# Decoder layer in fp32, one core: the last half batch of the feed-forward part in channel chunks and token tiles, the last batch's squares on another engine

## What is computed

```python
x = x + _L0_attn_ref(_layernorm(x), ...)
x = x + _L0_xattn_ref(ctx_1024, ctx_1024, _layernorm(x), ...)
x = x + _L0_ffn_ref(_layernorm(x), W_r, W_k, W_v, mu_r, mu_k)

# _L0_ffn_ref
x_prev = jnp.concatenate([jnp.zeros((B, 1, C), x.dtype), x[:, :-1, :]], axis=1)
xr = mu_r * x + (1.0 - mu_r) * x_prev
xk = mu_k * x + (1.0 - mu_k) * x_prev
r = jax.nn.sigmoid(jnp.einsum('btc,dc->btd', xr, W_r))
k = jnp.einsum('btc,dc->btd', xk, W_k)
k_act = jnp.square(jax.nn.relu(k))
out = r * jnp.einsum('btc,dc->btd', k_act, W_v)
```

## Time and profile before

| | us |
|---|---|
| median of 3 runs | 444.62 (443.23 to 445.12) |
| the profiled execution | 445.27 |
| its span, first to last instruction | 443.5 |
| TensorE busy | 427.9 |
| VectorE busy | 368.4 |
| ScalarE busy | 301.4 |
| GpSimd busy | 155.2 |

### The profile page before, as it was taken

How to read it: one execution, slowest core, us unless ns; L and a number is a source line. 1 busy time by engine, 2 the same in 40 slices (tenths; PEclk the granted TensorE clock), 3 DMA queues, 4 the chain that set the end, 5 groups by cost and what they waited for, 6 DMA issues and landing times.

```text
span 443.5 us, 8230 instructions
## 1 busy us (share of the span) xinstructions
PE 427.9 (96%) x2738; PEld 277.4 (63%) x2738; DVE 368.4 (83%) x672; ACT 301.4 (68%) x760; POOL 155.2 (35%) x200
## 2 busy tenths in 40 slices
PE   7999999999989999999999999999999999989888
PEld 5745463566546766576656685475665775568766
DVE  6788786979998889688999988799999888488875
ACT  4778986786796776657796577766877658428621
POOL 2171301137044343428242430734632532255410
PEclk9999999999999999999999999999999999979999
DMA  8668122715110002751103003443112000000001
GB/s 286 234 204 269 46 98 94 261 71 182 59 47 1 1 1 97 260 191 48 49 1 120 0 14 130 143 153 135 35 35 75 2 1 1 0 25 2 0 26 47
DMA packets 22177, 38.23 MB, mean 86 GB/s; under 512 B 2808, under 2 KB 7160, under 8 KB 21880
## 3 DMA queue, kind: packets, MB, share of 16 engines
q1 hardware_dynamic: 22136, 37.71, 25.1%
HBM read 23.02 MB, written 14.68 MB: 85 GB/s over the span
## 4 chain that ended last, share of the span: by engine, by line
PE 75%; DVE 9%; issue 6%; ACT 5%; POOL 3%; DMA 1%; SPq 0%; ACTq 0%; POOLq 0%; DVEq 0%
PE av_bank L913 22%; PE m_bank L845 8%; PE s_pair L899 8%; PE m_bank L849 6%; PE m_bank L1058 3%; ACT e_sb L1165 3%; PE m_bank L965 3%; DVE nmax L1369 3%; PE m_bank L1123 2%; PE m_bank L1070 2%; PE m_bank L1134 2%; PE m_bank L1145 2%; PE m_bank L983 2%; PE m_bank L930 1%; PE m_bank L1087 1%
## 5 line engine op out<-in xcount | busy, mean ns | idle before, releaser
L1165 ACT ACTIVATE e_sb<-s_pair,nmax 128x512 f32<-128x512 f32 x256 | 173.4, 690 | 61.6 <-DVE nmax L1369 59.8
L1369 DVE TENSOR_REDUCE nmax<-s_pair 128x2 f32<-128x1024 f32 x128 | 152.6, 1213 | 22.9 <-PE s_pair L899 21.8
L913 PE MATMUL av_bank<-e_sb,v_sb 128*64 128x512 f32 x512 | 119.0, 600 | 0.7 <-POOL v_sb L1649 0.7
L1649 POOL TENSOR_TENSOR v_sb<-v_sb,rsum 128x256 f32<-128x256 f32 x64 | 39.3, 617 | 140.4 <-DVE rsum L1377 135.7
L913 PEld LDWEIGHTS av_bank<-e_sb,v_sb 128*64 128x64 f32 x512 | 33.1, 136 | 61.6 <-issue 55.9
L899 PE MATMUL s_pair<-q_st,k_st 64*128 64x512 f32 x256 | 50.4, 457 | 3.3 <-ACT e_sb L1165 3.3
L1165 ACT ACTIVATION_READ_ACCUMULATOR e_sb<-s_pair,nmax 128x1 f32 x256 | 53.0, 207 | 0.0
L899 PEld LDWEIGHTS s_pair<-q_st,k_st 64*128 64x128 f32 x256 | 21.0, 184 | 36.7 <-ACT e_sb L1165 25.9
L1658 POOL TENSOR_TENSOR rstd<-veps,power 128x2 f32<-128x2 f32 x24 | 17.3, 719 | 58.6 <-DVE veps L1433 58.6
L845 PE MATMUL m_bank<-wo_hi,ot_hi 128*128 128x256 f32 x128 | 36.6, 291 | 0.0
L849 PE MATMUL m_bank<-wo_lo,ot_hi 128*128 128x256 f32 x128 | 34.9, 279 | 0.0
(11 more groups left out here) (182 smaller groups left out, 829.9 us busy)
## 6 DMA issues: line engine op xcount, KB each, us to landing
q_st<-q_parts SPq DMA_DIRECT2D x31, 256.0 KB, 3.4
k_st<-k_parts SPq DMA_DIRECT2D x31, 256.0 KB, 3.1
k_parts<-qkt_hi SPq DMA_DIRECT2D x7, 512.0 KB, 3.1
k_parts<-qkt_lo SPq DMA_DIRECT2D x7, 512.0 KB, 4.2
q_parts<-qkt_hi SPq DMA_DIRECT2D x8, 256.0 KB, 2.0
q_parts<-qkt_lo SPq DMA_DIRECT2D x8, 256.0 KB, 2.3
out<-x_sb SPq DMA_DIRECT2D x8, 256.0 KB, 2.2
x_sb<-in_x SPq DMA_DIRECT2D x3, 512.0 KB, 5.4
```

What stands on the lines that cost most here:

```text
L913: mm = pe.matmul(av_bank[n % AV_BANKS][64 * par:64 * par + 64, :], v_sb[:, m, 2 * p + par, :], e_sb[:, (4 * q + 2 * i + par) % E_RING, :], ...
L1165: act.activation(e_sb[:, g % E_RING, :], s_pair[k // 2][:, k % 2, :], ACT.Exp, bias=nmax[:, g % 8:g % 8 + 1], accum_out=esum[:, q % 4, k:k ...
L1369: dve.tensor_reduce(nmax[:, at:at + 2], s_pair[i][:, :, :], AX_X, ALU.max, negate=True)\
L1649: pool.tensor_tensor(v_sb[:, m:m + 2, 2 * p:2 * p + 2, :], v_sb[:, m:m + 2, 2 * p:2 * p + 2, :], rsum[:, q % 4, :].rearrange("p (m h) -> p ...
```

## The change

Seven edits, for batch 3, half 1 alone (`LAST_HALF`) unless said otherwise:

1. `t3` uses two banks, one for each channel chunk, and signals each when its two transposes are done; ScalarE copies each chunk by itself.
2. `mix` subtracts and mixes chunk by chunk, and signals `mixk_ready` after each; `mix_rec` signals `mixr_last` after each chunk.
3. `fk` uses two banks, one for each token tile, and has the input chunk c as its outer loop: 8 matmuls of 128 columns. Relu is applied tile by tile.
4. A new unit `frv` takes the place of `fr` and `fv` on TensorE: receptance then value products of tile 0, then of tile 1, in four banks.
5. tanh, gate, residual and store go tile by tile: two stores of 128 KB.
6. The squares of both halves of batch 3 are ACTIVATEs of Square on ScalarE, behind their relu; those of the other batches stay on GpSimd.
7. The seven warm-up matmuls at the end of TensorE's list go.

The diff, without the edits of the unit table (which drop the warm units at places 335 to 341, give `fr` and `fv` of (3, 1) no place of their own on TensorE, put `frv` at place 333, and drop the square units of batch 3 on GpSimd and VectorE):

```diff
@@ -29,7 +29,9 @@
 V_ON_DVE = (1, 3)
 X_TILES = 4
 
-BANKED = {"first", "t1", "qk", "v", "op", "t2", "kv", "kf", "z", "xs", "pt", "pv", "fc", "t3", "fr", "fk", "fv"}
+LAST_HALF = (B - 1, (1,))
+
+BANKED = {"frv", "first", "t1", "qk", "v", "op", "t2", "kv", "kf", "z", "xs", "pt", "pv", "fc", "t3", "fr", "fk", "fv"}
 
 
 UNITS = [
@@ -514,7 +510,9 @@
 
 def bank_units(name, b, args):
 
-    if name in ("xs", "z", "pv"):
+    if name == "frv":
+        return [(part, b, args + (t2,)) for t2 in range(2) for part in ("fr", "fv")]
+    if name in ("xs", "z", "pv") or (name in ("t3", "fk") and (b, args) == LAST_HALF):
         return [(name, b, args + (r,)) for r in range(2)]
     return [(name, b, args)]
 
@@ -722,6 +720,10 @@
 
             return xn[k > 1 or (b, half) == (0, 1)]
 
+        def is_last(b, half):
+
+            return (b, (half,)) == LAST_HALF
+
         def stacked(n):
 
             return n // STACK + (n % STACK != 0)
@@ -818,8 +820,14 @@
                 sp.dma_start(k_st[:, n % STACK, :].bitcast(F32), k_rows).then_inc(stack_in[1][n % STACK], 16)
 
             def fv(b, half):
+                t, at = b * NT + 2 * half, x_at(b, half)
+                if is_last(b, half):
+                    for t2 in range(2):
+                        sp.wait_ge(res_ready, 2 * b + half + 1 + t2)
+                        sp.dma_start(out.rearrange("(t p) d -> p t d", p=P)[:, t + t2, :], x_sb[:, at + t2, :])\
+                          .then_inc(res_out[half], 16)
+                    return
                 sp.wait_ge(res_ready, 2 * b + half + 1)
-                t, at = b * NT + 2 * half, x_at(b, half)
                 sp.dma_start(out.rearrange("(t p) d -> p t d", p=P)[:, t:t + 2, :],
                              x_sb[:, at:at + 2, :]).then_inc(res_out[half], 16)
 
@@ -834,8 +842,8 @@
             parts = {"load": load, "feat": lambda b: None, "x_load": x_load, "qk": qk, "ld": ld, "fv": fv}
             for _, name, b, args in order["sp"]:
                 parts[name](b, *args)
-            for half in range(2):
-                sp.wait_ge(res_out[half], 16 * B)
+            sp.wait_ge(res_out[0], 16 * B)
+            sp.wait_ge(res_out[1], 16 * (B + 1))
 
 
         @block.tensor
@@ -918,7 +926,9 @@
                 def t(b, half):
 
                     unit = (f"t{k}", b, (half,))
-                    wait_bank(pe, unit)
+                    units = bank_units(*unit)
+                    for used in units:
+                        wait_bank(pe, used)
                     i = k > 1
                     count = 2 * b + half if k == 1 else 4 * b + 2 * (k - 2) + half
 
@@ -927,9 +937,11 @@
                         pe.wait_ge(id_in, 16)
                     for c in range(DC):
                         for t2 in range(2):
-                            mm = pe.transpose(bank(unit)[:, c * HALF + t2 * P:c * HALF + (t2 + 1) * P],
+                            at = (c if len(units) == 1 else 0) * HALF + t2 * P
+                            mm = pe.transpose(bank(units[c % len(units)])[:, at:at + P],
                                               xn_at(k, b, half)[:, t2, c * P:(c + 1) * P], id_sb[:, :])
-                    mm.then_inc(filled[uses[unit][0]], 1)
+                        if len(units) == 2 or c == DC - 1:
+                            mm.then_inc(filled[uses[units[c % len(units)]][0]], 1)
                 return t
 
             def qk(b, c, o):
@@ -1126,6 +1138,20 @@
 
             def fk(b, half):
 
+                if is_last(b, half):
+                    units = bank_units("fk", b, (half,))
+                    for unit in units:
+                        wait_bank(pe, unit)
+                    for c in range(DC):
+                        pe.wait_ge(mixk_ready, 2 * b + half + 1 + c)
+                        for t2, unit in enumerate(units):
+                            for mc in range(DC):
+                                mm = pe.matmul(bank(unit)[:, mc * P:(mc + 1) * P], wffn_sb[:, 1, c, mc * P:(mc + 1) * P],
+                                               mix_k[:, c, t2 * P:(t2 + 1) * P],
+                                               start=((c, mc) == (0, 0)), stop=((c, mc) == (DC - 1, DC - 1)))
+                            if c == DC - 1:
+                                mm.then_inc(filled[uses[unit][0]], 1)
+                    return
                 unit = ("fk", b, (half,))
                 wait_bank(pe, unit)
                 pe.wait_ge(mixk_ready, 2 * b + half + 1)
@@ -1136,6 +1162,25 @@
                                        start=(c == 0), stop=(c == DC - 1))
                 mm.then_inc(filled[uses[unit][0]], 1)
 
+            def frv(b, half):
+
+                for unit in bank_units("frv", b, (half,)):
+                    wait_bank(pe, unit)
+                for t2 in range(2):
+                    tok = slice(t2 * P, (t2 + 1) * P)
+                    rec, val = ("fr", b, (half, t2)), ("fv", b, (half, t2))
+                    for c in range(DC):
+                        if t2 == 0:
+                            pe.wait_ge(mixr_last, 2 + c)
+                        mm = pe.matmul(bank(rec)[:, 0:D], mix_r[:, c, tok], wffn_sb[:, 0, c, :],
+                                       start=(c == 0), stop=(c == DC - 1))
+                    mm.then_inc(filled[uses[rec][0]], 1)
+                    pe.wait_ge(kact_ready, 2 * b + half + 1 + t2)
+                    for c in range(DC):
+                        mm = pe.matmul(bank(val)[:, 0:D], kact[:, c, tok], wffn_sb[:, 2, c, :],
+                                       start=(c == 0), stop=(c == DC - 1))
+                    mm.then_inc(filled[uses[val][0]], 1)
+
             def fv(b, half):
                 unit = ("fv", b, (half,))
                 wait_bank(pe, unit)
@@ -1316,6 +1361,13 @@
                                ACT.Copy).then_inc(oxt_hi_ready, 1)
 
             def t3(b, half):
+                if is_last(b, half):
+                    for c in range(DC):
+                        unit = ("t3", b, (half, c))
+                        wait_filled(act, unit)
+                        act.activation(xt3[:, c, 1 + HALF:1 + N], bank(unit)[:, 0:HALF], ACT.Copy)\
+                           .then_inc(emptied[uses[unit][0]], 1)
+                    return
                 unit = ("t3", b, (half,))
                 wait_filled(act, unit)
                 if b and half == 0:
@@ -1327,23 +1379,48 @@
 
             def fr(b, half):
 
-                unit = ("fr", b, (half,))
-                wait_filled(act, unit)
                 n = 2 * b + half
                 if n:
                     act.wait_ge(res_ready, n)
+                if is_last(b, half):
+                    for t2 in range(2):
+                        unit = ("fr", b, (half, t2))
+                        wait_filled(act, unit)
+                        act.activation(gate[:, t2, :], bank(unit)[:, 0:D], ACT.Tanh, scale=0.5)\
+                           .then_inc(emptied[uses[unit][0]], 1)
+                    return
+                unit = ("fr", b, (half,))
+                wait_filled(act, unit)
                 act.activation(gate[:, :, :], bank(unit)[:, :].rearrange("p (t d) -> p t d", t=2), ACT.Tanh,
                                scale=0.5).then_inc(emptied[uses[unit][0]], 1)
 
+            def fk_last(b, half):
+
+                units = bank_units("fk", b, (half,))
+                for t2, unit in enumerate(units):
+                    wait_filled(act, unit)
+                    act.activation(kact[:, :, t2 * P:(t2 + 1) * P], bank(unit)[:, 0:DC * P].rearrange("p (c n) -> p c n", c=DC),
+                                   ACT.Relu).then_inc(emptied[uses[unit][0]], 1)
+                for t2, unit in enumerate(units):
+                    wait_emptied(act, unit)
+                    act.activation(kact[:, :, t2 * P:(t2 + 1) * P], kact[:, :, t2 * P:(t2 + 1) * P], ACT.Square)\
+                       .then_inc(kact_ready, 1)
+
             def fk(b, half):
+                if (b, half) != (0, 0):
+                    pb, ph = (b, 0) if half else (b - 1, 1)
+
+                    wait_filled(act, ("fv", pb, (ph,)))
+                if is_last(b, half):
+                    fk_last(b, half)
+                    return
                 unit = ("fk", b, (half,))
                 wait_filled(act, unit)
-                if (b, half) != (0, 0):
-                    pb, ph = (b, 0) if half else (b - 1, 1)
-
-                    wait_filled(act, ("fv", pb, (ph,)))
                 act.activation(kact[:, :, :], bank(unit)[:, :].rearrange("p (c n) -> p c n", c=DC), ACT.Relu)\
                    .then_inc(emptied[uses[unit][0]], 1)
+                if b == B - 1:
+                    wait_emptied(act, unit)
+                    act.activation(kact[:, :, :], kact[:, :, :], ACT.Square).then_inc(kact_ready, 1)
 
             parts = {"first": first, "cut": cut, "feat": feat, "t1": t1, "qk": qk, "v": v, "kf": kf_, "t2": t2, "z": z, "xs": xs, "pt": pt,
```

(50 more changed lines are left out.)

11 lines of the change are left out of this document (2 added, 9 removed).

## The result

| | before | changed |
|---|---|---|
| median | 444.71 us (443.23 to 445.53, 5 runs) | 442.91 us (441.47 to 443.14, 5 runs) |
| ratio | | 0.9947, 95% interval 0.9923 to 0.9972 |
| the profiled execution | 445.27 us | 441.47 us |
| its span | 443.5 us | 439.7 us |
| mean granted clock | 0.992 | 0.999 |

The changed kernel is 0.53% faster; the forecast was 442.3 us in a range of 441.3 to 443.9. The two profiled executions differ by 3.8 us, more than the medians by far, so they can't be subtracted as they stand. VectorE's last normalisation starts at 429.32 in the old one and at 427.82 in the new one: 1.50 us of the difference lies ahead of it, where of all the edits only half 0's square on ScalarE (427.40) stands, and the normalisation does not wait for that.

The account below looks back on a forecast made before the run. The last half batch's chain of waits through VectorE, TensorE, ScalarE and the final store sets the end. Terms -0.70 - 0.85 + 0.20 - 0.55 - 0.38 = -2.28 us off the median 444.62 give 442.3 us, range 441.3 to 443.9.

Parts of the forecast that it names:

- normalisations, to the transposes: VectorE's last two normalisations, freed from GpSimd's square, take 0.74 instead of 1.44 us, so transposes start earlier: -0.70 us.
- value products of half 0, to the key products: TensorE's last key products follow half 0's value products with no idle time, mixes being ready: -0.85 us.
- the new wait: TensorE waits for the last half's first square, now behind only one tile of receptance products: +0.2 us, between 0 and 0.5.
- gate and residual of the last piece: VectorE's last tile takes two 128x256 operations, 0.87 us where it was 1.43: -0.55 us.
- store, to the end of the span: Last store moves 128 KB instead of 256 KB: -0.38 us, at least 0 if only the fixed part counts.
- Squares on ScalarE: Last batch's half-0 square moves from GpSimd into ScalarE's idle time: cost zero, gain 0.70 us on VectorE's normalisations.
- Key products of 128 columns: Last half's key products on TensorE: 16 records of 128 columns take 1.73 us, as 8 of 256 did.
- rival (b): Small pieces do not pay: open weight loads (+1.3 us at most) or handovers about 1 us more; 443.5 us, chance 0.13.
- The mixes come in time: VectorE's key mixes of both chunks are ready 0.25 us before TensorE asks for each, so key products run without idle time.
- rival (a): Square needs another ScalarE table load between relu and square of the last half: +1.28 us, 443.6 us, chance 0.08.
- rival (c): TensorE's clock falls to the 1.2 GHz level in the tail: +5.2 us, 447.5 us, chance 0.05.
- Rival (d): GpSimd's square was not the collision, so VectorE's normalisations stay at 1.44 us: sum -1.6, 443.0 us, chance 0.06.

Follow-up runs that it names:

- `square_pool`: Changed kernel with the square of half 0 of the last batch back on GpSimd: tail 12.55 us against 11.88 in the changed kernel.
- `whole_mix`: Changed kernel with the channel chunks undone (one bank and copy for the transposes, mixes signalled whole): tail 12.76 us, 0.88 more than the changed kernel.

## Why the prediction was right, step by step

All times from the start of the last normalisation:

| term | forecast | before | changed | measured |
|---|---|---|---|---|
| normalisations, to the transposes | -0.70 | 1.58 | 0.88 | -0.70 |
| value products of half 0, to the key products | -0.85 | 2.58 | 1.73 | -0.85 |
| key products, to the last gate | +0.20 | 5.48 | 5.69 | +0.21 |
| gate and residual of the last piece | -0.55 | 1.41 | 0.88 | -0.53 |
| store, to the end of the span | -0.38 | 2.66 | 2.24 | -0.42 |
| sum | -2.28 | | | -2.29 |

The sum of the forecast is the tail's (0.01 us more lies between the transposes and the value products). One of its terms came out right in part by luck, the +0.20 of the new wait. The forecast had TensorE wait 0.19 us for the first square. It waited 0.08, mostly because the handover from ScalarE took 0.05 us where the forecast had 0.14, and the first group after the wait took 0.11 us longer, a cost that the forecast named and left out. The end before is 1.41 us by the earlier trace rows, whose gate starts at 439.43, and not the 1.43 of the forecast, so that term should read -0.54. The half store saved more than the 0.38 us of the sum, and more than the estimate of 0.30 beside it.

Squares on ScalarE: right in place and size, and undone or done alone they move the tail by 0.67 and 0.70 us. Key products of 128 columns: 1.79 us for 16 records, 1.81 for the 8 of before; the bound of 1.3 us for open weight loads was not touched, so rival (b) falls. The mixes come in time: forecast slack 0.25 us for each chunk, measured 0.15 for each (430.60 and 431.46, plus 0.14, against 430.89 and 431.75); the rest went into the first handover from ScalarE to VectorE, 0.12 us where the forecast had 0.02. Square loads no table, so rival (a) falls. The 2.7 us that the Trainium skill, ScalarE: Activation LUTs, Table sets, budgets for a switch is not tested here, as no switch took place; the one load in this trace took 1.28 us, and what stands around a load in a switch no run shows. The clock held in the tail until the last value products (1.00 from 427 to 436.5 us): rival (c) falls for the tail, though its mechanism is alive 30 us upstream. Rival (d) falls by `square_pool`.

What I had not priced is the state of the rest of the program. The forecast was laid against a median, 444.62, whose own runs differ by 1.9 us; I gave that 0.6 us in the range and no cause. Part of it is the clock upstream, in steps of 0.8 to 1.4 us by the table, and part is the unexplained spread ahead of 390 us. Together they give the profiled pair its 3.8 us: 2.3 in the tail, 2.4 by the clock, less the 0.9 us by which the changed kernel's execution came later to 390 us. The medians moved by 1.8 and then 2.0 us where the tail moved by 2.3. The first difference can't be taken apart, since the clocks of the old kernel's executions in it are not on record. In the second both medians are executions at 0.996, so what is missing there is the scatter within a step (before: 443.3 to 443.7 us even at full clock, 444.1 to 445.0 at 0.996), not the clock. The forecast of 442.3 us is 0.6 us under the measured median: 0.5 is the smaller move, 0.1 that the median before is 444.71 over its five runs. Of the 2.22 us that it names as the least that can be told, the 2.30 of the tail lie just past and the 1.80 of the medians inside: on which side the result fell is chance, although the interval of the ratio stands clear of 1.

## What to carry to other kernels

When a change touches one stage, compare the stage from a common event to the end, and compare totals only at equal granted clock (and even then they scatter by up to 1 us here). Splitting a unit pays where another engine waits for its first part (the gap of 0.85 us, the last store), and costs where it shortens the cover of a later wait (0.19 us here). Before moving an operation off GpSimd for its speed, look for the VectorE operation that starts beside it: the gain here was not GpSimd's 1.04 us but the 0.70 us that VectorE stood still.

## What the runs showed of the hardware

- A VectorE tensor_scalar of 128x256 from and to SBUF waits out a GpSimd tensor_tensor in SBUF that started 0.07 to 0.08 us earlier, and ends 0.14 to 0.16 us after it: two of them take 0.73 us alone, 1.01 beside 0.61 us of GpSimd, 1.44 beside 1.04. The second of the two takes its usual 0.40 us.
- Square of 128x512 in SBUF took 0.63 us on ScalarE, 0.69 on VectorE and 1.04 on GpSimd, and on ScalarE it ran with exp, tanh, relu and copy on one table load.
- fp32 matmuls of 128 columns with a 128x128 weight load for each record ran at 0.11 us a record (16 in 1.79 us), half of the 0.22 us of 256 columns; the weight loads of 0.19 us stayed hidden.
- A stall on TensorE cost its length and 0.07 to 0.11 us more at the restart (four records in 0.97 instead of 0.86 us; the key products' records end to end 2.02 instead of 1.95 us in `whole_mix`).
- The granted clock fell to 1.2 GHz, in some executions, in one stretch where TensorE had gaps of 0.3 to 0.9 us and was busy for 9.6 to 10.1 of 12 us; with gaps of 0.3 to 0.8 us it held in others. It cost about 1.4 or 2.4 us. Four matmuls with no use, 0.43 us each, held it in 12 runs of 12; with one of the old ones taken away it was lost in 8 of 8; the kernel before, beside them, kept it in 9 of 15.
